# Two-layer graph network: edges of later windows from where their rows' own begin, fields from a table that ScalarE copies

## Chip, cores and metric

One core of one Trainium2 chip. The metric is the device time of one execution in microseconds, lower is better.

## What is computed

80,000 edges (src, dst, weight) join 2,500 nodes of 1,024 features. dst is sorted and dense at low numbers. Two layers, each with a layer norm in front:

```python
dst = jnp.minimum((2500 * uniform(80000) ** 2.0).astype(int32), 19999)   # then sorted
h = jnp.maximum(_layernorm(x, axis=-1), 0.0)
x = x + segment_sum((h @ W0)[src] * edge_weight[:, None], dst, 2500)
h = jnp.maximum(_layernorm(x, axis=-1), 0.0)
# layer 2: graph convolution with self loops, norm = deg**-0.5 [row] * deg**-0.5 [col], h2 = h @ W1.T + b
x = x + segment_sum(norm[:, None] * h2[col], row, 2500)
```

## The kernel before

Nothing is gathered by edge. Both layers multiply by matrices of nodes by nodes that the kernel builds itself: A with the sums of the weights of the edges from src to dst, and C with the counts of edges. They are built by matmuls of one-hot matrices. 128 edges make a *chunk* (625 of them, one edge a partition). A *window* is 4 rows of dst (640 windows, the last ones empty), 4 windows are a *quad* (160), 8 quads a tile of 128 rows (20). To *touch* a window with a chunk means one matmul of 128 by 128 by 240 columns: its left side marks for each edge which of the 128 (row, part of src) combinations of the window it has, its right side has the count and the two halves of the weight at the edge's place among 80. 8 touches are a *step*, with two buffers. A chunk belongs to a window only in part: what lies outside matches nothing.

How many chunks a window is touched with is fixed (`chunks_of`, `steps_of`): 32, 16, 8, 8 in quad 0, 8 in quads 1 to 3, 4 up to quad 31 (`UQ`), then 2 (`UL`). Where a window's edges reach over more chunks than that, `further` makes passes of 4 more chunks each, in a branch that the table `wtab` opens (first chunk, passes, passes before it, sum of the quad).

For a step of before:
- GpSimd, `fields` (L611, L613): for each window in turn it loads the first chunk from the table and copies the chunks' fields from `etab` (key, place, two halves of the weight) to `fbuf`, each twice, less the window's base. `sum_counts` (L627) adds the counts of a quad to the degrees.
- VectorE, `one_hots` (L863, L865, L868, L869): two comparisons with `iota_r` and two products.
- TensorE, `step` through `multiply` (L1379).
- ScalarE, `window_out` (L1154 to L1156), evacuates a quad from PSUM; VectorE, `second_part` (L920, L923), makes the low half of A.
- SyncE, `store_quad` (L413, L415), stores counts and both parts of A; `load_weights` (L424) loads a tile of A transposed, two DMAs, after the stores of all its quads.

There are two stages of this. First come the 20 *support* tiles (`support`, L1367, h @ W0, 48 products a tile), in which quads 0 to 15 are woven in from tile 4 on (`STEP0`, `STEPS_AT`: after which of the eight k-parts a step comes). VectorE, ScalarE and GpSimd have their order for a tile written out by hand; in tiles 4 to 7 ScalarE and GpSimd also split the second weights in blocks of which four belong to a tile (`W1_AT`, `split_block`, L1170, L1174, L636), stored by SP. Then 18 tiles of the aggregation (`dense`, L1433, 120 products of 512 columns a tile, 15 beside each quad) go with quads 16 to 159, which are two tiles ahead of their use. Two tiles are one turn of the loops of TensorE, VectorE and SyncE (two tiles are written out before them), one tile is a turn of ScalarE's. At a tile's start SP waits until the last quad is stored, then issues `load_weights`; the next quad's store is behind it in SP's queue, and ScalarE may evacuate a quad only when the store of the one two before has landed. TensorE may start a quad when the one two before is evacuated. VectorE's order in a quad is one-hots, second part of the quad before, `further`.

At the head VectorE makes the table for all 640 windows in nine passes on one partition (L822 to L832). L1460 spreads two fp32 rows over the partitions. L907 is the comparison of a further pass, L785 the low part of the support. After the loop come two tiles of aggregation without quads, and then the second layer (L1525, L1580), which the change doesn't touch.

## Time and profile before

| | |
|---|---|
| median of three runs | 1647.43 us (1643.34, 1647.43, 1656.27) |
| profiled execution | 1643.0 us |
| its span | 1641.3 us |
| TensorE busy | 1507.0 us (92%) |
| VectorE busy | 1064.6 us (65%) |
| GpSimd busy | 596.6 us (36%) |
| ScalarE busy | 443.1 us (27%) |
| support tiles end | at 334.3 us |
| last quad's step ends | at about 1010.4 us |

Busy times are of one execution. Matmuls are pipelined, so that a group's mean length is longer than its distance from one to the next. Times in the text without another word count from the span's start.

### The profile page before, as it was taken

The page shows a single profiled execution, that of the slowest core. Times are in us where ns is not written, and L with a number is a line of the kernel's source. Part 1 is how long each engine was busy: PE and PEld are TensorE (multiplying, and loading weights), DVE is VectorE, ACT ScalarE, POOL GpSimd, SP SyncE. Part 2 cuts the span into 40 slices and gives each one's busy share as a digit, 9 for nine tenths or more (in the row PEclk, how much of TensorE's full clock was granted, in tenths as well). Part 3 has the DMA queues.
Part 4 walks back from the last instruction along what each step waited for, and adds up shares of the span by engine and source line. Part 5 has one row for each costly group of instructions (what it writes and reads, how often), then busy time and mean ns, then how long its engine had stood idle before and what let it go on. Part 6 is the DMA issues. An engine that isn't in the chain of part 4 may idle for free.

```text
span 1641.3 us, 28252 instructions
## 1 busy us (share of the span) xinstructions
PE 1507.0 (92%) x7964; PEld 804.4 (49%) x7965; DVE 1064.6 (65%) x1917; ACT 443.1 (27%) x855; POOL 596.6 (36%) x1530
## 2 busy tenths in 40 slices
PE   3978999967889999999999999989999999999997
PEld 2444555534444545445444554334645545546455
DVE  5887764448867778778687785389555456355442
ACT  5745544312122222222222221171202103002000
POOL 1135543435656778667677774000000000000000
PEclk9989999988989999999999999999999999999999
DMA  7202421174556666656665656571331412403102
GB/s 279 104 26 68 147 58 33 25 157 97 110 119 142 151 146 139 143 131 157 136 151 130 151 135 160 180 281 32 125 102 51 120 56 89 128 11 122 55 1 75
DMA packets 411488, 185.71 MB, mean 113 GB/s; under 512 B 376875, under 2 KB 393791, under 8 KB 411342
## 3 DMA queue, kind: packets, MB, share of 16 engines
q1 hardware_dynamic: 411342, 184.03, 42.7%
q8 instruction: 59, 0.97, 0.2%
q14 instruction: 87, 0.71, 0.2%
HBM read 76.45 MB, written 77.11 MB: 94 GB/s over the span
## 4 chain that ended last, share of the span: by engine, by line
PE 58%; DVE 12%; SPq 9%; DMA 7%; issue 6%; ACT 3%; DVEq 1%; POOL 1%; ACTq 1%; POOLq 0%
PE pair L1525 20%; PE pair L1580 13%; PE pair L1367 9%; PE pair L1433 9%; SPq L424 6%; PE pair L1379 5%; DMA a_scratch<-area 5%; DVE slots L868 2%; DVE slots L865 2%; DVE slots L869 1%; DVE area L920 1%; DVE slots L863 1%; SPq L415 1%; SPq L445 1%; DMA wstage<-c_scratch 1%
## 5 line engine op out<-in xcount | busy, mean ns | idle before, releaser
L1433 PE MATMUL pair<-h,area 128*128 128x512 f16 x2400 | 548.1, 382 | 4.3 <-issue 3.9
L1433 PEld LDWEIGHTS pair<-h,area 128*128 128x128 f16 x2400 | 232.8, 98 | 266.1 <-issue 17.2
L1525 PE MATMUL pair<-area,h 128*128 128x500 f16 x1600 | 341.9, 376 | 6.4 <-DVE h L1042 6.4
L1379 PE MATMUL pair<-slots 128*128 128x240 f16 x1640 | 205.9, 272 | 76.6 <-DVE slots L869 58.8
L611 POOL CAST fbuf<-etab 128x12 f16 (+2 forms) x644 | 205.8, 320 | 174.6 <-DVE slots L869 106.6
L1525 PEld LDWEIGHTS pair<-area,h 128*128 128x128 f16 x1600 | 156.1, 98 | 191.5 <-issue 11.7
L1379 PEld LDWEIGHTS pair<-slots 128*128 128x128 f16 x1640 | 158.4, 99 | 138.6 <-DVE slots L869 65.6
L1154 ACT ACTIVATE area<-pair 128x320 f32<-128x320 f32 x160 | 69.9, 437 | 542.7 <-PE pair L1379 317.7
L613 POOL TENSOR_TENSOR fbuf<-etab,negbase 128x4 f16 (+3 forms) x644 | 211.0, 328 | 0.5 <-issue 0.5
L1580 PE MATMUL pair<-wmat,area 128*125 128x512 f16 x960 | 209.0, 379 | 0.0
L863 DVE TENSOR_TENSOR slots<-iota_r,fbuf 128x640 f16<-128x640 f16 x204 | 106.0, 519 | 142.9 <-POOL fbuf L613 85.4
L627 POOL TENSOR_TENSOR deg_acc<-deg_acc,area 128x320 f32<-128x320 f32 x160 | 145.0, 906 | 93.7 <-ACT area L1156 93.3
L1580 PEld LDWEIGHTS pair<-wmat,area 128*125 128x125 f16 x960 | 130.6, 136 | 75.5
L865 DVE TENSOR_TENSOR slots<-iota_r,fbuf 128x1024 f16<-128x1024 f16 x204 | 144.4, 708 | 0.0
L1309 ACT ACTIVATE area<-pair,sc 128x500 f16<-128x500 f32 x40 | 27.1, 677 | 385.2 <-PE pair L1525 385.2
L920 DVE SCALAR_TENSOR_TENSOR area<-pair,area 128x320 f16<-128x320 f32 x160 | 77.5, 484 | 81.9 <-ACT area L1156 81.6
L1367 PE MATMUL pair<-wmat,agg_t 128*128 128x512 f16 x480 | 112.7, 388 | 5.2 <-DVE wmat L778 4.0
L1082 DVE SCALAR_TENSOR_TENSOR area<-pair,sc,area 128x500 f16<-128x500 f32 x40 | 29.1, 738 | 128.3 <-ACT area L1309 128.2
L1367 PE MATMUL pair<-wmat,xt 128*128 128x512 f16 x480 | 110.0, 382 | 1.4 <-issue 1.4
L868 DVE TENSOR_TENSOR slots<-slots,fbuf 128x640 f16<-128x640 f16 x204 | 109.3, 536 | 0.0
L923 DVE TENSOR_TENSOR area<-area 128x320 f16<-128x320 f16 x160 | 101.4, 634 | 5.5
L869 DVE TENSOR_TENSOR slots<-slots,fbuf 128x640 f16<-128x640 f16 x204 | 104.1, 510 | 0.0
(195 smaller groups left out, 1117.5 us busy)
## 6 DMA issues: line engine op xcount, KB each, us to landing
c_scratch<-area SPq DMA_DIRECT2D x160, 160.0 KB, 2.3
a_scratch<-area SPq DMA_DIRECT2D x320, 80.0 KB, 2.3
xt<-x_scratch SPq DMA_DIRECT2D x20, 500.0 KB
out_x<-xt SPq DMA_DIRECT2D x20, 500.0 KB
xt<-in_x SPq DMA_DIRECT2D x19, 512.0 KB, 3.7
x_scratch<-xt SPq DMA_DIRECT2D x19, 512.0 KB, 3.3
wstage<-c_scratch SPq DMA_DIRECT2D x17, 500.0 KB, 4.5
slots<-c_scratch SPq DMA_DIRECT2D x17, 500.0 KB, 4.6
```

The lines of the kernel that those rows point to most:

```text
L611: pool.tensor_copy(fbuf[:, s, 1:F, at].rearrange("p f u d -> p u f d"), twice(etab_c[:, bass.ds(c, u), 1:F], [P, u, F - 1, 2])).then_inc(s ...
L613: pool.tensor_tensor(fbuf[:, s, 0, at], twice(etab_c[:, bass.ds(c, u), 0], [P, u, 2]), twice(negbase[:, bass.ds(v0 + w, 1)], [P, u, 2]), A ...
L627: pool.tensor_tensor(deg_acc[:], deg_acc[:], c_stage(s), ALU.add).then_inc(win_sum, 1)
L863: nc.vector.tensor_tensor(part(hot(s), M0, SB), columns(8, SB), by_touch(s, 1, 8, SB), ALU.is_equal).then_inc(hots_plain, 1)
L865: nc.vector.tensor_tensor(part(hot(s), 0, P), columns(8, P), by_touch(s, 0, 8, P), ALU.is_equal)
L868: nc.vector.tensor_tensor(part(hot(s), W0C, SB), part(hot(s), M0, SB), by_touch(s, 2, 8, SB), ALU.mult)
L869: nc.vector.tensor_tensor(part(hot(s), W1C, SB), part(hot(s), M0, SB), by_touch(s, 3, 8, SB), ALU.mult).then_inc(hots_ready, 1)
L1367: last = pe.matmul(dest[:, half * H:(half + 1) * H], h_t(t)[:, q, k, :], wmat[:, r, k, half * H:(half + 1) * H], start=k == q == r == 0, s ...
L1379: return pe.matmul(dest, touches[:, t, 0:P], touches[:, t, P:CS], start=first, stop=last, skip_group_check=True)
L1433: last = pe.matmul(sum_pair(e)[:, half * H:(half + 1) * H], wts(e)[:, q, k, :], hpart(k, r)[:, half * H:(half + 1) * H], start=k == q == r ...
L1525: ins = pe.matmul(sums_of(c, f), hpart(k, q)[:, f * P:(f + 1) * P], counts, start=first and q == 0, stop=last and q == 1, skip_group_check ...
L1580: last = pe.matmul(out_pair(m)[0:RW, half * H:(half + 1) * H], agg_of(k, q)[:, b * RW:(b + 1) * RW], wmat[:, r, k, half * H:(half + 1) * H ...
```

## The change

Windows of quads 16 to 63 are touched with 2 sets of 128 edges and those of quads 64 to 159 with 1, where the sets begin at the window's own first edge and not at a chunk's border: partition p takes the edge of the first chunk where that one is at or after the window's first row, and else that of the next chunk. A step is then one quad (16 to 63) or two (64 to 159). The fields of all these touches are made once, as a table `own` of 128 partitions by touches, four fields: matmuls of the edges' fields with one-hot matrices of the chunk numbers (`chunk_hot`, made at tile 6) give the fields of the second and third chunk and of the one that leads; VectorE chooses with predicated copies. TensorE does this in the support tiles named by `OWN_AT` and `SCRATCH_AT`, between its k-parts (`tables`), into TP; ScalarE copies TP out (`tables_out`) ahead of its weight blocks and of `window_out`; VectorE selects (`own_select`). A window with edges left over is forced out of the table and done by `further` passes alone (`select_windows`). The table of passes is made for 64 windows at the head and for the others at tile 16 (`later_windows`). In the loop ScalarE copies a step's fields from `own` into `fbuf`, in two copies of two fields each, a step ahead (`own_step`). GpSimd writes fields only for quads 0 to 15 and, at the head, makes three half-precision copies of the natural fields. The first `load_weights` moves from tile 12 to 17 of the support tiles. The loops of VectorE and TensorE are each two, up to quad 63 and from 64. The diff at its core:

```diff
-    U0, UH, UP, UL = (32, 16, 8, 8), 8, 4, 2
+    U0, UH, UP = (32, 16, 8, 8), 8, 4
     HQ = 4
     PRE = 2
     PQ = PRE * QPT
-    UQ = 4 * QPT
+    UA, UB, QB = 2, 1, 64
     BT = 4
     CS = P + 3 * SB
...
+    VA, VB = 4 * PQ, 4 * QB
+    NA = NW - VA
+    NT = UA * (VB - VA) + UB * (NW - VB)
+    V_HALF = (NA // 2, NA // 2)
...
+        ROW_AT, HOTS_AT, SELECT_AT, TABLE_AT = 5, 6, 9, 16
+        OWN_AT = {7: (0, 0), 8: (0, 1), 10: (1, 0), 11: (1, 1), 12: (2, 0), 13: (2, 1), 14: (3, 0), 15: (3, 1)}
+        SCRATCH_AT = sorted([ROW_AT, SELECT_AT, *OWN_AT])
...
-                if w == QPT:
+                if w + STEP0 == TABLE_AT + 1:
+                    sp.wait_ge(own_ready, len(OWN_AT))
+                    sp.wait_ge(table_ready, 2)
...
-            for t in range(4):
+            for t in range(2):
                 h_left(t)
-            for t in range(4, STEP0 + 2):
+            pool.wait_ge(scans_ready, 2)
+            pool.wait_ge(fields_ready, 2)
+            pool.tensor_copy(key_hi, field[0]).then_inc(nat_ready, 1)
+            pool.tensor_copy(from_h, field[1]).then_inc(nat_ready, 1)
+            pool.wait_ge(nat_ready, 1)
+            pool.tensor_tensor(key_lo, field[0], key_hi, ALU.subtract).then_inc(nat_ready, 1)
+            for t in range(2, STEP0 + 2):
...
-                    fields_of(w + 1)
+                    if w + 1 < PQ:
+                        fields_of(w + 1)
                     if w > 0:
                         sum_counts(w - 1, (w - 1) % 2)
-            for n in range(PQ, UQ):
-                if n + 1 < UQ:
-                    fields_of(n + 1)
-                else:
-                    step_loop(UQ, 0)
-                sum_counts(n - 1, (n - 1) % 2)
-            with pool.Fori(UQ // 2, NQ // 2 - 1) as i:
+            sum_counts(PQ - 1, 1)
+            with pool.Fori(PQ // 2, NQ // 2) as i:
                 for s in range(2):
-                    step_loop(i * 2 + s + 1, 1 - s)
-                    sum_counts(i * 2 + s - 1, 1 - s)
-            step_loop(NQ - 1, 1)
-            for n in range(NQ - 3, NQ):
-                sum_counts(n, n % 2)
+                    sum_counts(i * 2 + s, s)
 
             def self_loops(c, j):
 
...
+            def passes(a, b, count, cum, spare, start=None):
+
+                n = b - a
+                whole = spare[:, 0:n].bitcast(i32)
+                chain(nc.vector.tensor_scalar(whole, count, float(BT - 1), None, ALU.add))
+                chain(nc.vector.tensor_scalar(tab[:, 1, a:b], whole, 2, None, ALU.logical_shift_right))
+                chain(nc.vector.tensor_copy(spare[:, 0:n], tab[:, 1, a:b]))
+                chain(nc.vector.tensor_tensor_scan(cum, spare[:, 0:n], spare[:, 0:n], 0.0, ALU.add, ALU.bypass))
+                if start is not None:
+                    chain(nc.vector.tensor_scalar(cum, cum, start, None, ALU.add))
+                chain(nc.vector.tensor_scalar(tab[:, 3, a:b], cum, 1.0, None, ALU.add))
+                quads = spare[:, n:n + n // 4]
+                chain(nc.vector.tensor_reduce(quads, spare[:, 0:n].rearrange("o (g w) -> o g w", w=4), AX.X, ALU.add))
+                chain(nc.vector.tensor_copy(tab[:, 3, a:b].rearrange("o (g w) -> o w g", w=4)[:, 0, :], quads))
+                nc.vector.tensor_tensor(tab[:, 2, a:b], cum, spare[:, 0:n], ALU.subtract).then_inc(table_ready, 1)
+
             dve.wait_ge(wrow_in, 16 * NB)
-            lo_row = wrow.rearrange("o (v a) -> o a v", a=2)[:, 0, 0:NW]
-            n_row = wrow.rearrange("o (v a) -> o a v", a=2)[:, 1, 0:NW]
-            tab = wtab.rearrange("o (v a) -> o a v", a=4)
-            cum = wcum[:, 0:NW]
-
-            chain(nc.vector.tensor_scalar(wint[:, 0:NW], n_row, float(BT - 1), None, ALU.add))
-            chain(nc.vector.tensor_scalar(tab[:, 1, :], wint[:, 0:NW], 2, None, ALU.logical_shift_right))
-            chain(nc.vector.tensor_copy(n_row, tab[:, 1, :]))
...
+            def own_hots(k, s, used):
+                dve.wait_ge(own_fields, 2 * (k - PRE_STEPS) + 2)
+                one_hots(k, s, used)
...
+                    if chunks == UA:
+                        own_hots(n + PRE_STEPS - PQ, q % 2, n - 1 + PRE_STEPS - PQ)
+                    elif q % 2 == 0:
+                        own_hots((td + PRE) * 4 + q // 2 + QB // 2 + PRE_STEPS - PQ, q // 2 % 2, steps_used(n - 2))
...
+            def own_select(t):
+
+                f, half = OWN_AT[t]
+                at = slice(half * V_HALF[0], (half + 1) * V_HALF[0])
+                dve.wait_ge(own_copied, scratch_uses(t) + 1)
+                two = VB - VA if half == 0 else 0
+                pairs = own[f][:, 0:UA * two].rearrange("p (v u) -> p u v", u=UA)
+                singles = own[f][:, UA * (VB - VA):NT][:, 0 if half == 0 else V_HALF[0] - (VB - VA):]
+                singles = singles[:, 0:V_HALF[0] - two]
+                lead = from_lead[:, 0:V_HALF[0]]
+                mask = from_first[:, at]
+                if f == 0:
+                    chain(nc.vector.tensor_scalar(mask, lead, 0.0, None, ALU.is_ge))
+                    for chunk, a, b in ((pairs[:, 1], 0, two), (singles, two, V_HALF[0])):
+                        if a < b:
+                            out = left_over[:, at][:, a:b]
+                            chain(nc.vector.scalar_tensor_tensor(out, chunk, 0.0, mask[:, a:b], ALU.is_ge, ALU.mult))
+                            chain(nc.vector.scalar_tensor_tensor(out, chunk, P / 2, out, ALU.is_lt, ALU.mult))
+                    if half == 0:
+                        chain(nc.vector.tensor_scalar(sums_row, tab[:, 1, VA:NW], -1.0, 0.0, ALU.add, ALU.max))
+                    rest = left_over[0:1, at]
+                    nc.vector.tensor_tensor(rest, rest, sums_row[:, at], ALU.add).then_inc(left_ready, 1)
+                if two:
+                    nc.vector.copy_predicated(singles, mask[:, two:V_HALF[0]], lead[:, two:V_HALF[0]])
+                    chain(nc.vector.copy_predicated(pairs[:, 1], mask[:, 0:two], pairs[:, 0]))
+                    last = nc.vector.copy_predicated(pairs[:, 0], mask[:, 0:two], lead[:, 0:two])
+                else:
+                    last = nc.vector.copy_predicated(singles, mask, lead)
+                last.then_inc(own_ready, 1)
+
+            def select_windows():
+
+                dve.wait_ge(own_copied, scratch_uses(SELECT_AT) + 1)
...
+            def select_windows():
+
+                dve.wait_ge(own_copied, scratch_uses(SELECT_AT) + 1)
+                dve.wait_ge(own_ready, 2)
+                chain(nc.vector.tensor_scalar(forced, forced, 0.0, 50000.0, ALU.is_gt, ALU.mult))
+                pairs = own[0][:, 0:UA * (VB - VA)].rearrange("p (v u) -> p u v", u=UA)
+                for u in range(UA):
+                    nc.vector.scalar_tensor_tensor(pairs[:, u], pairs[:, u], 10000.0, forced[:, 0:VB - VA],
+                                                   ALU.min, ALU.add)
+                singles = own[0][:, UA * (VB - VA):NT]
+                chain(nc.vector.scalar_tensor_tensor(singles, singles, 10000.0, forced[:, VB - VA:NA], ALU.min, ALU.add))
+                for u, a, b in ((UA, 0, VB - VA), (UB, VB - VA, NA)):
+                    chain(nc.vector.tensor_scalar(sums_row[:, a:b], tab[:, 1, VA + a:VA + b], float(u), None, ALU.add))
+                chain(nc.vector.scalar_tensor_tensor(sums_row, forced[0:1, :], 0.0, sums_row, ALU.is_gt, ALU.mult))
+                chain(nc.vector.tensor_copy(tab[:, 1, VA:NW], sums_row))
+
+            def later_windows():
+                chain(nc.vector.tensor_copy(wcum[:, 0:NA], tab[:, 1, VA:NW]))
+                passes(VA, NW, wcum[:, 0:NA], wcum[:, 0:NA], wtmp, top[0:1, 10:11])
 
             hots_of(0)
...
+                if w + STEP0 == HOTS_AT:
+                    chunk_one_hots()
+                if w + STEP0 in OWN_AT:
+                    own_select(w + STEP0)
+                if w + STEP0 == SELECT_AT:
+                    select_windows()
+                if w + STEP0 == TABLE_AT:
+                    later_windows()
...
+            with dve.Fori(1, ONE_FROM) as i:
                 tile(i, 0)
                 tile(i, 1)
+
+            dve.wait_ge(step_used, steps_used(QB - 1))
+            with dve.Fori(ONE_FROM, T // 2 - 1) as i:
+                tile(i, 0, UB)
+                tile(i, 1, UB)
             chain(nc.vector.tensor_reduce(sel[:], ident[:].rearrange("p (r k) -> p k r", r=R), AX.X, ALU.add))
...
+            def own_step(k, s):
+
+                act.wait_ge(hots_ready, k - 1)
+                at = bass.ds((k - PRE_STEPS) * 8, 8)
+                act.activation(fbuf[:, s, 0:2], twice(own_k[:, :, at], [P, 2, 8, 2]), ACT.Copy).then_inc(own_fields, 1)
+                act.activation(fbuf[:, s, 2:4], twice(own_w[:, :, at], [P, 2, 8, 2]), ACT.Copy).then_inc(own_fields, 1)
+
+            def tile(td, chunks=UB, last=False):
                 for q in range(QPT):
                     n = QPT * (td + PRE) + q
-                    window_out(n, q % 2, steps_before(n + 1))
+                    if chunks == UA:
+                        own_step(n + 1 + PRE_STEPS - PQ, 1 - q % 2)
+                    elif q % 2 == 0 and not (last and q == QPT - 2):
+                        own_step((td + PRE) * 4 + q // 2 + 1 + QB // 2 + PRE_STEPS - PQ, 1 - q // 2 % 2)
+                    window_out(n, q % 2, steps_used(n + 1))
 
...
+            def tables_out(t):
+
+                act.wait_ge(own_sums, scratch_uses(t) + 1)
+                if t not in OWN_AT:
+                    dest = chunk_row if t == ROW_AT else forced
+                    act.activation(dest[:, 0:512], TP[:, 0:512], ACT.Copy)
+                    act.activation(dest[:, 512:NA], TP[:, 512:NA], ACT.Copy).then_inc(own_copied, 1)
+                    return
+                f, half = OWN_AT[t]
+
+                need(act, own_ready, own_at(t) - 1)
+                n, two = V_HALF[half], VB - VA if half == 0 else 0
+                act.activation(from_lead[:, 0:n], TP[:, 0:n], ACT.Copy)
+                if two:
+                    pairs = own[f][:, 0:UA * two].rearrange("p (v u) -> p u v", u=UA)
+                    act.activation(pairs[:, 1], TP[:, n:n + two], ACT.Copy)
+                    act.activation(pairs[:, 0], TP[:, H:H + two], ACT.Copy)
+                a = UA * (VB - VA) + (0 if half == 0 else V_HALF[0] - (VB - VA))
+                act.activation(own[f][:, a:a + n - two], TP[:, H + two:H + n], ACT.Copy).then_inc(own_copied, 1)
+
...
+            act.wait_ge(table_ready, 2)
+            act.wait_ge(own_ready, len(OWN_AT))
+            own_step(PRE_STEPS, 0)
+            with act.Fori(0, QB // QPT - PRE) as td:
+                tile(td, UA)
+            with act.Fori(QB // QPT - PRE, T - PRE - 1) as td:
                 tile(td)
-            with act.Fori(UQ // QPT - PRE, T - PRE) as td:
-                tile(td)
...
+            def own_step(k, s, u, pair, half=0):
+
+                pe.wait_ge(hots_ready, k + 1)
+                for t in range(4 * u):
+                    last = multiply(hot(s), half * 4 + t, win(pair, t // u), first=t // u % 2 == t % u == 0,
+                                    last=t % u == u - 1)
+                last.then_inc(step_used, 1)
+
...
+            def tables(t):
+
+                if t + 1 < T:
+                    pe.wait_ge(ht_ready, 2 * t + 4)
+
+                need(pe, own_copied, scratch_uses(t))
+                if t == ROW_AT:
+                    pe.wait_ge(wrow_in, 16 * NB)
+                    pe.matmul(TP[:, 0:512], ones[0:1, :], lo_row[:, VA:VA + 512], start=True, stop=True)
+                    pe.matmul(TP[:, 512:NA], ones[0:1, :], lo_row[:, VA + 512:NW], start=True,
+                              stop=True).then_inc(own_sums, 1)
+                    return
+                if t == SELECT_AT:
+                    pe.wait_ge(left_ready, 2)
+                    pe.matmul(TP[:, 0:512], ones_h, left_over[:, 0:512], start=True, stop=True)
+                    pe.matmul(TP[:, 512:NA], ones_h, left_over[:, 512:NA], start=True, stop=True).then_inc(own_sums, 1)
+                    return
+                f, half = OWN_AT[t]
+                pe.wait_ge(chunk_hots, 1)
+                pe.wait_ge(nat_ready, 3)
+                n = V_HALF[half]
+                at = half * V_HALF[0]
+                two = VB - VA if half == 0 else 0
+                for g, dest, width in ((0, TP[:, 0:n], n), (1, TP[:, H:H + n], n), (2, TP[:, n:n + two], two)):
+                    if not width:
+                        continue
+                    if f == 0:
+                        pe.matmul(dest, ones_h[0:1, :], neg_row[:, at:at + width], start=True, stop=False)
+                    for i, by_chunk in enumerate(own_parts[f]):
+                        for j in range(J):
+                            last = pe.matmul(dest, by_chunk[:, j * P:(j + 1) * P], chunk_hot[:, j - g + 2, at:at + width],
+                                             start=f > 0 and i == j == 0, stop=i == len(own_parts[f]) - 1 and j == J - 1)
+                last.then_inc(own_sums, 1)
+
             def further(n, pair):
...
+                    if k == 5 and t in SCRATCH_AT:
+                        tables(t)
...
+            with pe.Fori(0, ONE_FROM) as i:
+                tile(i, 0, UA)
+                tile(i, 1, UA)
+            with pe.Fori(ONE_FROM, T // 2 - 1) as i:
+                tile(i, 0, UB)
+                tile(i, 1, UB)
```

## Rows read from the trace of the kernel before

**Rows 1.** The page's first line: the span and its instructions
```profile
span 1641.3 us, 28252 instructions
```

**Rows 2.** Windows by stage: start:end and length, busy us (records) per engine, clock, DMA
```profile
193.30:334.30 141.00, 141.00 (x865) 77.72 (x863) 70.63 (x151) 64.02 (x97) 54.85 (x108) 1.00 0.18 38
334.30:471.10 136.80, 104.28 (x593) 58.51 (x593) 100.56 (x206) 23.00 (x62) 70.88 (x192) 0.89 0.59 128
...
588.00:1010.40 422.40, 396.53 (x2219) 212.68 (x2217) 321.96 (x625) 105.20 (x288) 300.78 (x854) 1.00 0.63 143
```

**Rows 3.** Groups by line: count, busy us and mean ns, idle before them
```profile
L1379 PE MATMUL pair<-slots 128*128 128x240 f16 x1640 | 205.9, 272 | 76.6 <-DVE slots L869 58.8 <-DVE area L920 6.6 <-DVE slots L912 6.1
...
L865 DVE TENSOR_TENSOR slots<-iota_r,fbuf 128x1024 f16<-128x1024 f16 x204 | 144.4, 708 | 0.0
...
L863 DVE TENSOR_TENSOR slots<-iota_r,fbuf 128x640 f16<-128x640 f16 x204 | 106.0, 519 | 142.9 <-POOL fbuf L613 85.4 <-issue 34.5 <-PE pair L1379 19.8
...
L1460 PE MATMUL pair<-area,ones 1*128 1x512 f32 (+1 forms) x8 | 4.3, 716 | 3.7 <-ACT etab L1227 3.7
...
L825 DVE TENSOR_TENSOR_SCAN area<-area 1x640 f32<-1x640 f32 x1 | 1.5, 1478 | 0.0
...
L907 DVE TENSOR_TENSOR slots<-iota_r,fbuf 128x512 f16<-128x512 f16 x2 | 0.9, 426 | 0.0
```

**Rows 4.** TensorE in order of time, the loop: start us, length us
```profile
550.26 0.98 PE L1379 MATMUL pair<-slots 128*128 128x240 f16 x8
...
554.31 0.98 PE L1379 MATMUL pair<-slots 128*128 128x240 f16 x8
555.13 3.40 PE L1433 MATMUL pair<-h,area 128*128 128x512 f16 x15
...
575.48 0.99 PE L1379 MATMUL pair<-slots 128*128 128x240 f16 x8 [0.72 <-DVE slots L869]
...
588.05 0.98 PE L1379 MATMUL pair<-slots 128*128 128x240 f16 x8
...
611.83 0.99 PE L1379 MATMUL pair<-slots 128*128 128x240 f16 x8 [1.80 <-DVE slots L869]
```

**Rows 5.** Chain of waits, 720 to 800: start us, length us, what
```profile
728.51 3.87 issue
...
768.71 0.37 SPq L413
...
772.05 2.80 SPq L424
...
774.99 2.90 SPq L424
...
779.28 2.33 DMA a_scratch<-area
...
786.63 0.99 PE pair L1379 x8
```

**Rows 6.** TensorE in order of time, from the loop's first tiles
```profile
341.00 3.36 PE L1379 MATMUL pair<-slots 128*128 128x240 f16 x16 [6.57 <-DVE area L920]
...
376.07 3.51 PE L1379 MATMUL pair<-slots 128*128 128x240 f16 x16 [13.04 <-DVE slots L869]
...
455.48 0.98 PE L1379 MATMUL pair<-slots 128*128 128x240 f16 x4 [6.07 <-DVE slots L912]
```

**Rows 7.** SyncE's queue in order of time, same stretch
```profile
351.44 16.16 SPq L445 DMA_TRANSPOSE wmat<-w_scratch  x2
```

**Rows 8.** TensorE in order of time, support tiles
```profile
93.03 2.75 PE L1367 MATMUL pair<-wmat,agg_t 128*128 128x512 f16 x12 [1.19 <-DVE h L785]
...
185.91 1.78 PE L1379 MATMUL pair<-slots 128*128 128x240 f16 x8 [3.41 <-DVE slots L869]
```

**Rows 9.** ScalarE in order of time, support tile 5
```profile
133.41 0.70 ACT L1170 ACTIVATE h<-h,sc 128x512 f32<-128x512 f32 x1
```

**Rows 10.** VectorE in order of time, a late support tile
```profile
306.82 0.49 DVE L863 TENSOR_TENSOR slots<-iota_r,fbuf 128x640 f16<-128x640 f16 x1 [7.07 <-POOL fbuf L613]
```

175 lines of the change are left out of this document (105 added, 70 removed).

## The prediction

> **What bounds the kernel now.** I read the windows by stage first, then the groups by line, then TensorE's order of time, and last the chain of waits inside one tile. The page's own execution spans 1641.3 us [rows 1] and took 1643.0 us, so what lies around the span is 1.7 us. The median of the three runs shown is 1647.43, 4.4 above it. TensorE (PE) is the engine to follow. In support tiles 8 to 19 it is busy for all of 141.00 us [rows 2]: whatever is added on PE there is added to the time. From 334.3 to 471.1, where quads 16 to 35 are done, it is busy 104.28 of 136.80 us [rows 2]: here other things bound it. A step is 8 matmuls of 240 columns. The groups show 1640 of them [rows 3]: 204 steps, and 2 further passes of 4.
>
> In the loop a quad costs PE 0.82 us for the step and 3.24 us for 15 products: steps start at 550.26, 554.31, and the products begin at 555.13 [rows 4]. Pure pace would be 4.06 us a quad. But from the last quad of a tile (554.31) to the fifth of the next (575.48) it takes 21.17 us, not 5 x 4.06 = 20.3, and the next time (588.05 to 611.83) 23.78 us [rows 4]. The chain of waits tells why [rows 5]: the last quad's store is issued at 768.71, then two transposing loads hold the SP queue 2.80 and 2.90 us, only then goes the next quad's store, which lands after 2.33 us; ScalarE's evacuation of the third quad has waited for that landing, VectorE's second part and the one-hots for the fifth quad follow it, and PE starts at 786.63. The last quad's step had begun some 21.2 us before that. None of this chain is made shorter by fewer matmuls. In the other tile of each pair VectorE also pays 3.87 us of "issue" as its loop goes back [rows 5].
>
> **The change part by part.**
>
> *Fewer steps.* Before: 44 steps up to quad 15, 2 x 16 for quads 16 to 31, 128 for the rest, 204. After: 44 + 48 (quads 16 to 63) + 48 (one step for two quads, 64 to 159) = 140. It takes away 64 steps: 52 us of PE at 0.82 us, and on VectorE 64 times some 2 us (519 and 708 ns for the two comparisons [rows 3], and two products of the first one's size, which overlap a little). How much of that is on the path is told by stage.
>
> *Quads 16 to 35.* The stage is 136.80 us [rows 2]. (a) PE first stands 6.57 us before 341.00 [rows 6]; VectorE has then made both steps' one-hots of quad 16 before it finishes quad 15. With one step this is 1.6 to 2.0 us less; I take 1.6. (b) Then SP issues the transposes, the two of the second weights alone 16.16 us from 351.44 [rows 7], and PE stands 13.04 us before 376.07 [rows 6]. That chain keeps its length; it ends 1.6 earlier, at 374.4. PE comes to it sooner and waits longer, for nothing gained. (c) From there before goes at 5.5 to 6 us a quad, VectorE-bound with two steps each (2 x 2 us and the second part). After, it goes as the later loop does: three quads of 4.06 and about 1.5 for the cold clock, 388.1; one chain of 21.2, three quads, one more chain: quad 36 begins at 442.7, against 471.1 before. (d) In this is a further pass: the row of 4 matmuls at 455.48 had PE idle 6.07 us [rows 6], and only two such passes are in the trace (L907, x2 [rows 3]), one in quad 0, which stays. The reference's own inputs give at most 222 edges in a window of quads 16 to 63 and 113 in one of quads 64 and up, so that 256 and 128 slots counted from the window's own first edge hold them: no later pass is left. Sum: 28.4 us less. Bounds: 18 (if only (a), the pass and half of the VectorE time come off) and 34.
>
> *Quads 36 to 63.* Same steps, same chain. GpSimd's copies no longer run beside VectorE's one-hots, and ScalarE gets two 32-element copies a quad, which I put at 0.2 us each (a third to a half of its 320-element copy); it waits most of the time. They are queued ahead of the evacuation of the quad before, and they wait for one-hots that are one quad older, which are done. The cover is ScalarE's idle time; without it each quad would be 0.4 us longer. Change 0, bounds -4 and +6.
>
> *Quads 64 to 159.* A quad falls from 4.06 to 3.65 us (half a step). Outside the chain there are three quads a tile, 12 tiles: 36 x 0.41 = 14.8 us less. Inside the chain nothing: five quads now need only 18.25 us and PE stands 3 us in a 21.2 us chain. Where VectorE's loop goes back the chain starts by VectorE's clock, and the last quad's step is now 0.41 us later with respect to it, so it takes about 24.5: 5 x 0.65 = 3.3 us more. One of the old back-branches (quad 63 to 64) becomes the passage from one loop into the next, which I take as 2.7 us less. That is 14.2 us less. Against it stand PE's longer idle times. After 3.41 us of idling the 8 matmuls at 185.91 took 1.78 us instead of 0.98 [rows 4, 8]: TensorE's 1.2 GHz level instead of 2.4. Tiles at the back-branch would have gaps of 2.3 and 4.0 us; I charge 1.1 us in each of 5: 5.5. Net 9 us less. Bounds: 15 less, and with 1.6 us in all 12 tiles, 5 more.
>
> By the Trainium skill (Runtime: NRT & Kernel Launch, section Instruction fetch mechanics) a taken branch to a page outside the two held ones must fetch it first, and straight running does not. The trace agrees in so far as VectorE's long loop shows 3.87 us at its start. By that rule falling out of one loop into the next costs nothing; were it wrong, the 2.7 us would go and the sum be 14.
>
> *Tiles 4 to 19, what is added.* The tables are made by one-hot matmuls in TP: 22 x 288 + 11 x 192 columns for support tile 7, 22 x 288 for 8, then 3 x (20 x 288 + 5 x 192) for 10 to 15, 34,944 columns. At 0.82 us for 8 x 240 columns [rows 4] that is 14.9 us, of it 3.6 in tile 7, 2.7 in 8 and 8.6 in 10 to 15; 0.3 in 9. Tile 5 has 576 fp32 columns at the rate of L1460, whose eight records take 4.3 us for 1250 columns [rows 3]: 2.0 us. These sums stand on PE in the stage where it is never idle. More comes from ScalarE's order. It reads the tables after PE's sixth part of the tile, and its blocks of the second weights (tiles 4 to 7) stand behind that. In tile 5 the blocks began at 133.41 [rows 9]. Now ScalarE must wait for PE to about 139.1 and copy to 139.9, 6.5 us later; GpSimd, the next fields and PE follow, about 4.8 us of it reaching PE. In tile 7 it waits for 3.6 us of matmuls as well, so that PE's second step of tile 8, at 185.91 before [rows 8], comes some 10.6 us late. With tile 8's own 2.7, 0.3 and 8.6 it is 22 us.
> VectorE's selects, one-hots of chunk numbers and the later windows' table are hidden: it idles 7.07 us in such a tile [rows 10], the largest block (nine passes over 576 elements on one partition, of which the scan is 1478 ns for 640 [rows 3]) some 9 us, with 3 to 4 us of slack at PE. In tiles 10 to 15, though, the select waits for ScalarE's copy near the end of the tile and two one-hot sets stand behind it; I find only about 1 us to spare there. Every us more would be PE's in up to 8 tiles.
> At the head the table of the first 64 windows replaces one of 640, about 6 us less on VectorE, but PE waited for it only 1.19 us at 93.03 [rows 8]: about 2 less. Net 20 us more; bounds 11 (the PE columns of tiles 8 to 15 alone) and 45.
>
> **Sum.** -28.4 + 0 - 9 + 20 = -17: 1643.0 - 17 = 1626 against the profiled execution, 1630 against the median. I say 1628.
>
> **The rivals.** About 1% is what a measurement of this kernel tells from no change.
> 1. *The tables hold the support tiles up.* VectorE's select, behind ScalarE's copy, makes the next one-hots late, 3 us in each of 8 tiles (24 us), and the wait in tile 7 is longer by 5; also the idle times cost the clock in every late tile (nothing gained there). 20 + 29 - 28 + 0 = 21 more: 1664. For it: 1 us of slack by my count, and an order with four engines in it. Against: VectorE's 7.07 us idle. It decides from about 2.5 us a tile. 0.15.
> 2. *What is saved late is eaten by waits and the clock.* PE's time in quads 64 to 159 doesn't change, since the chain through the transposes is what counts, and the tables cost 25: -28 + 25 = -3, 1640. For it: [rows 5]. 0.27.
> 3. *The chain shrinks with the load.* If with GpSimd out the stores and the second part come sooner and PE alone sets the pace, quads 64 to 159 take 96 x 3.65 = 350 us plus 6 stalls of 2.3 instead of the 422.40 of [rows 2]: 1643 + 20 - 28 - 58 = 1577. Against: every link of it is on SP, DMA and ScalarE, and stays. 0.05.
> 4. *It doesn't do what it says*: windows overflow and take further passes, 8 to 10 us each as at 455.48. The counts above exclude it nearly: 0.01.
> My forecast has 0.52.
>
> **How the numbers follow.** The forecast's own range is 1612 to 1643; taking in most of rival 2 and the bounds of the tables' cost, 1603 to 1655. The forecast lies at the 1% mark, and a little over half of it and all of rival 3 are beyond: faster 0.46; same 0.39; slower 0.15 from rival 1.
>
> **What would show it.** Right: 140 steps (1124 matmuls of 240 columns with the pass that stays), one L907 pass, no GpSimd casts after tile 19; the support tiles 8 to 19 ending about 20 us later; quad 36 about 8 us earlier than before; 39 us less matmul time in quads 64 to 159, but more idling of PE there, and the stretch from a tile's last quad to the next one's fifth still 21 to 25 us. Wrong: support tiles longer than 14.5 us each (rival 1), a stretch under 20 us (rival 3), or ScalarE late with the fields, seen as VectorE waiting for it ahead of the one-hots.

## The result, and the profile after

The changed kernel takes 1671.27 us (median of four runs, 1666.7 to 1672.5) against 1648.75 for the kernel before (median of four): a ratio of 1.0136, with a 95% interval of [1.0111, 1.016]. I had said 1628, in 1603 to 1655. It is slower, and outside the range. The profiled execution took 1672.5 us.

The first lines of the page of the changed kernel:
```profile
span 1670.7 us, 24358 instructions
## 1 busy us (share of the span) xinstructions
PE 1496.5 (90%) x7584; PEld 776.4 (46%) x7585; DVE 953.0 (57%) x1710; ACT 472.7 (28%) x1075; POOL 262.9 (16%) x384
```
The work did shrink: VectorE from 1064.6 to 953.0 us, GpSimd from 596.6 to 262.9. The span grew by 29.4 us.

Windows by stage of the kernel before, where quads 36 to 63, quads 64 to 159 and the rest are cut apart (columns as in [rows 2]); [rows 2] has the two stages ahead of them:
```profile
471.10:593.40 122.30, 115.35 (x645) 61.82 (x643) 91.46 (x179) 30.68 (x84) 88.52 (x250) 1.00 0.62 139
593.40:1009.40 416.00, 391.25 (x2185) 209.65 (x2186) 320.01 (x621) 104.11 (x285) 298.95 (x847) 1.00 0.63 143
1009.40:1641.30 631.90, 612.90 (x2871) 318.16 (x2869) 335.69 (x495) 113.13 (x173) 15.21 (x25) 0.99 0.30 97
```
And of the changed kernel, support tiles 8 to 19, quads 16 to 35, 36 to 63, 64 to 159, the rest:
```profile
193.30:360.20 166.90, 161.80 (x1003) 91.30 (x1003) 100.31 (x210) 72.36 (x123) 51.89 (x115) 0.98 0.23 58
360.20:472.10 111.90, 87.18 (x461) 46.47 (x460) 67.96 (x135) 28.07 (x106) 18.34 (x20) 0.88 0.70 151
472.10:601.90 129.80, 120.06 (x644) 63.49 (x645) 94.33 (x182) 37.13 (x140) 27.87 (x28) 0.96 0.58 134
601.90:1037.10 435.20, 374.28 (x1807) 179.30 (x1806) 220.81 (x427) 114.64 (x377) 85.98 (x95) 0.94 0.61 137
1037.10:1670.70 633.60, 612.12 (x2867) 317.61 (x2865) 335.83 (x495) 113.25 (x173) 14.46 (x25) 0.99 0.30 97
```

| stage | before | after | difference | forecast |
|---|---|---|---|---|
| support tiles end | 334.3 | 360.2 | +25.9 | +20 |
| quads 16 to 35 | 136.8 | 111.9 | -24.9 | -28.4 |
| quads 36 to 63 | 122.3 | 129.8 | +7.5 | 0 |
| quads 64 to 159 | 416.0 | 435.2 | +19.2 | -9 |
| the rest | 631.9 | 633.6 | +1.7 | 0 |

The largest miss is where I expected a gain. In quads 64 to 159 TensorE's busy time fell by only 17 us (391.25 to 374.28), not by the 39 of 48 steps, and its granted clock from 1.00 to 0.94. The groups by line in that stretch, kernel before:
```profile
L1433 PE MATMUL pair<-h,area 128*128 128x512 f16 x1425 | 323.3, 379 | 2.5 <-issue 2.1
L1379 PE MATMUL pair<-slots 128*128 128x240 f16 x760 | 93.7, 266 | 23.4 <-DVE slots L869 23.3
...
L865 DVE TENSOR_TENSOR slots<-iota_r,fbuf 128x1024 f16<-128x1024 f16 x95 | 64.9, 684 | 0.0
```
and changed kernel (L1649 are the products of the aggregation, L1553 the steps, L919 the larger comparison):
```profile
L1649 PE MATMUL pair<-h,area 128*128 128x512 f16 x1426 | 342.7, 395 | 7.5 <-issue 7.5
...
L1553 PE MATMUL pair<-slots 128*128 128x240 f16 x381 | 57.6, 276 | 53.4 <-DVE slots L923 53.4
...
L919 DVE TENSOR_TENSOR slots<-iota_r,fbuf 128x1024 f16<-128x1024 f16 x47 | 38.7, 824 | 0.0
```
The steps cost 36 us less, but the idle time before them grew by 30 (23.4 to 53.4), and the same products, none added, took 19 us more (323.3 to 342.7). TensorE in order of time shows both at one place, the fifth quad of a tile, changed kernel:
```profile
721.14 0.57 PE L1553 MATMUL pair<-slots 128*128 128x240 f16 x4
721.55 3.40 PE L1649 MATMUL pair<-h,area 128*128 128x512 f16 x15
728.54 0.98 PE L1553 MATMUL pair<-slots 128*128 128x240 f16 x4 [3.58 <-DVE slots L923]
729.86 5.77 PE L1649 MATMUL pair<-h,area 128*128 128x512 f16 x15 [0.34 <-issue]
735.47 0.57 PE L1553 MATMUL pair<-slots 128*128 128x240 f16 x4
735.88 3.40 PE L1649 MATMUL pair<-h,area 128*128 128x512 f16 x15
```
A quad goes at 3.65 us as forecast (0.41 for half a step and 3.24 for the products). Then TensorE stands 3.58 us, and the 15 products behind the pause take 5.77 us, where they take 3.40 elsewhere: most of them at the 1.2 GHz level. It idles 3.2 to 4.2 us at the fifth quad of each of the 12 tiles, and 1.5 to 1.9 us where the loop goes back. From the fifth step to the sixth it takes 5.3 to 7.0 us. That is 1.7 to 3.4 us over the pace, in every tile. From 728.50 to 735.40 the granted clock is 0.55 of full speed, from 735.40 to 742.00 it is 1.00. Behind the 1.5 to 1.9 us at the loop's turn the 15 products take 3.41 us, as elsewhere.

What it waits for is the chain I had read in [rows 5], in the same place, changed kernel's chain of waits:
```profile
712.86 2.90 SPq L470
...
715.89 2.82 SPq L470
...
720.11 3.08 DMA a_scratch<-area
...
724.00 0.45 ACT area L1290
724.48 0.50 DVE area L982
...
726.33 0.17 DVE slots L919
726.50 1.10 issue
...
728.08 0.41 DVE slots L923
728.49 0.05 issue
728.54 0.98 PE pair L1553 x4
```
Two transposing loads, the next quad's store, ScalarE's evacuation, VectorE's second part and one-hots, the step. The last quad's step before the loads to the fifth quad's step: 21.6 to 22.2 and 24.7 to 25.2 us in the two kinds of tile (without and with the jump back of VectorE's loop), where it was 21.3 to 21.5 and 23.7 to 24.4 in the kernel before. The chain is a little longer, and the work beside it is less. Two of its links grew. The comparison of L919 takes 1.35 us (0.17 and the 1.10 of issue behind it in this view, until the next one can start) where L865 took 0.68. And in the tiles without the jump the store behind the two loads lands after 3.0 to 3.1 us (3.08 above) where it took 2.3 to 2.4 (2.33 in [rows 5]); with the jump it takes 2.0 to 2.1 in both kernels. Why that store became slower is open.

### The profile page after: what moved, and what is told of

Same layout as the page of the kernel before. It is cut to its first block, busy times and chain, and to the rows that moved or that the text cites. A ratio compares the mean times of both kernels' runs of the same rounds, so it can differ in the third digit from the quotient of the medians.

```text
span 1670.7 us, 24358 instructions
## 1 busy us (share of the span) xinstructions
PE 1496.5 (90%) x7584; PEld 776.4 (46%) x7585; DVE 953.0 (57%) x1710; ACT 472.7 (28%) x1075; POOL 262.9 (16%) x384
## 4 chain that ended last, share of the span: by engine, by line
PE 60%; SPq 10%; DVE 9%; DMA 8%; issue 7%; ACT 4%; DVEq 1%; ACTq 1%; POOL 0%; POOLq 0%
PE pair L1744 20%; PE pair L1799 12%; PE pair L1541 10%; PE pair L1649 10%; SPq L470 6%; DMA a_scratch<-area 5%; PE pair L1553 4%; DVE area L982 1%; DVE slots L922 1%; DVE slots L923 1%; SPq L461 1%; DVE slots L919 1%; SPq L459 1%; DMA wstage<-c_scratch 1%; SPq L493 1%
## 5 line engine op out<-in xcount | busy, mean ns | idle before, releaser
L1649 PE MATMUL pair<-h,area 128*128 128x512 f16 x2400 | 571.4, 394 | 9.1 <-issue 9.0
L1649 PEld LDWEIGHTS pair<-h,area 128*128 128x128 f16 x2400 | 240.0, 101 | 288.6 <-issue 55.2
L1553 PE MATMUL pair<-slots 128*128 128x240 f16 x1124 | 152.4, 276 | 110.3 <-DVE slots L923 93.3
L1553 PEld LDWEIGHTS pair<-slots 128*128 128x128 f16 x1124 | 109.9, 100 | 165.8 <-DVE slots L923 112.8
L917 DVE TENSOR_TENSOR slots<-iota_r,fbuf 128x640 f16<-128x640 f16 x140 | 74.5, 532 | 92.7 <-issue 54.4
L919 DVE TENSOR_TENSOR slots<-iota_r,fbuf 128x1024 f16<-128x1024 f16 x140 | 110.1, 786 | 0.0
L985 DVE TENSOR_TENSOR area<-area 128x320 f16<-128x320 f16 x160 | 76.9, 481 | 5.5
L923 DVE TENSOR_TENSOR slots<-slots,fbuf 128x640 f16<-128x640 f16 x140 | 75.5, 540 | 0.0
L1541 PEld LDWEIGHTS pair<-wmat,agg_t 128*128 128x128 f16 x480 | 47.8, 101 | 57.2 <-issue 10.0
L922 DVE TENSOR_TENSOR slots<-slots,fbuf 128x640 f16<-128x640 f16 x140 | 74.1, 529 | 0.0
L1541 PEld LDWEIGHTS pair<-wmat,xt 128*128 128x128 f16 x480 | 46.7, 99 | 53.9 <-issue 4.2
```

The lines of the kernel that those rows point to most:

```text
L919: nc.vector.tensor_tensor(part(hot(s), 0, P), columns(8, P), by_touch(s, 0, 8, P), ALU.is_equal)
L922: nc.vector.tensor_tensor(part(hot(s), W0C, SB), part(hot(s), M0, SB), by_touch(s, 2, 8, SB), ALU.mult)
L923: nc.vector.tensor_tensor(part(hot(s), W1C, SB), part(hot(s), M0, SB), by_touch(s, 3, 8, SB), ALU.mult).then_inc(hots_ready, 1)
L985: nc.vector.tensor_tensor(a_stage(s)[:, 1], a_stage(s)[:, 1], a_stage(s)[:, 2], ALU.add).then_inc(win_lo, 1)
L1541: last = pe.matmul(dest[:, half * H:(half + 1) * H], h_t(t)[:, q, k, :], wmat[:, r, k, half * H:(half + 1) * H], start=k == q == r == 0, s ...
L1553: return pe.matmul(dest, touches[:, t, 0:P], touches[:, t, P:CS], start=first, stop=last, skip_group_check=True)
```

## The experiments

Late stage means quads 64 to 159. Each ratio is to the kernel before as timed beside that run; 2 and 11 are edits of the kernel before, all others of the changed one. Idle is TensorE's idle time before steps in it, and a product's mean length is that of the 512-column products there.

| kernel | median us | ratio | late stage us | idle us | product ns |
|---|---|---|---|---|---|
| before | 1646 to 1649 | 1 | 416.0 | 23.4 | 379 |
| changed | 1671.27 | 1.0136 | 435.2 | 53.4 | 395 |
| 1 more products ahead of the wait | 1637.44 | 0.9932 [0.9909, 0.9955] | 406.8 | 33.3 | 387 |
| 2 the same in the kernel before | 1648.08 | 1.0001 [0.999, 1.0012] | | | |
| 3 steps' matmuls twice | 1675.04 | 1.0167 [1.015, 1.0185] | 438.9 | 33.1 | 388 |
| 4 weight blocks first | 1654.04 | 1.0037 [1.0019, 1.0055] | 435.6 | | |
| 5 degrees cut | 1650.31 | 1.0023 [1.0007, 1.0039] | 425.5 | 42.8 | 395 |
| 6 no copies | 1668.42 | 1.013 [1.01, 1.0161] | 435.5 | 49.6 | 399 |
| 7 one-hots a quad earlier | 1619.21 | 0.9842 [0.9813, 0.9871] | 383.7 | 21.1 | 386 |
| 8 idle time filled | 1652.57 | 1.0038 [1.0024, 1.0052] | 417.4 | 14.5 | 384 |
| 9 experiments 4 and 7 | 1605.77 | 0.9748 [0.9731, 0.9764] | | | |
| 10 one-hots early in all quads | 1600.69 | 0.9723 [0.9706, 0.9739] | 389.9 | 25.3 | 387 |
| 11 one-hots early in the kernel before | 1702.94 | 1.0346 [1.0327, 1.0365] | | | |
| 12 and the loop's end | 1586.34 | 0.9632 [0.9616, 0.9648] | 380.8 | 17.7 | 385 |

**1 and 2. Another division of the products over the quads.** Quads 0 to 3 of a tile get 18 of the 120 products, 4 to 6 get 10, the last 18, so that there is more work for TensorE while the chain runs. Once in the changed kernel (1), once in the kernel before (2).

```diff
-        SUMS_AT = [15 * q for q in range(QPT + 1)]
+        SUMS_AT = [0, 18, 36, 54, 72, 82, 92, 102, 120]
```

> The changed kernel with the 120 products of a tile divided 18, 18, 18, 18, 10, 10, 10, 18 over its eight quads in place of 15 each: work moves into the five quads that lie in the stretch from a tile's last quad to the next tile's fifth, out of the three behind it. Theory A (the stretch of 22 to 25 us is set by the chain through store and transposes, TensorE idles 3.4 to 4.2 us in it and then runs products at the 1.2 GHz level): the idling goes, the clock stays up, and a pair of tiles in quads 64 to 159 goes from 73.2 us to about 62 to 65; 1671 becomes 1580 to 1610. Theory B (the late stage is slower because each quad waits for ScalarE's copies and VectorE, and the idling costs nothing by itself): a quad with more products is only longer, the pair stays at 71 to 75 and the time within 1% of 1671.

> The kernel before with the same division of the products. Theory A: here TensorE idles only about 1 to 2 us in the stretch and has 32.5 us of its own work in a tile of 35; it gains less, 1 to 2 us a tile, 15 to 35 us in all, and ends up slower than the changed kernel with the same division. Theory B: no gain, and the changed kernel stays behind it by the 20 to 25 us of now.

Measured: the changed kernel gains 34 us by it, the kernel before nothing (1648.08, ratio 1.0001 [0.999, 1.0012]). With this division the order of the two turns round: the changed one is 11 us ahead. So a good part of the loss is waiting that work from elsewhere in the tile can fill. Both gains are smaller than theory A had them (to 1580 to 1610, and 15 to 35 us for the kernel before). In both kernels the idle time moved to the first quad of the loop's turn (in the kernel before TensorE stood 3.24 us before 594.69 and 3.71 before 666.47, in the changed one 3.30 to 3.69 us at that place), with a slow stretch behind it; why it moved there I didn't follow further.

**3. The removed matmuls put back.** The steps of quads 64 to 159 do their 4 matmuls a quad twice.

```diff
-                for t in range(4 * u):
+                for t in list(range(4 * u)) * (2 if u == UB else 1):
```

> The changed kernel with the four matmuls of each quad from 64 on done twice over (the first of a bank starts its sums anew, so the sums are the same): the matmuls that the change took away come back, 96 x 0.41 = 39 us of TensorE, all else stays. Theory A: they fill the wait, TensorE idles about 1.5 to 2 us at a tile's fifth quad in place of 3.5 to 4.2, keeps 2.4 GHz more often, and quads 64 to 159 take 420 to 430 us in place of 435: with 4 x 96 more matmuls the kernel is 5 to 15 us faster. Theory B, or if the clock costs nothing: 36 quads lie outside the stretch and cost 0.41 each, 15 us slower.

Measured: 39 us of matmuls came back, and the late stage grew by 3.7 us (435.2 to 438.9). A tenth of their length: nine tenths of what the change takes from TensorE there lay in waits and in slow products. The time is 3.8 us longer, between the two expectations (5 to 15 us faster, 15 slower).

The run says more than that. In this stage it has all the matmuls of the kernel before (2185 records on TensorE in both), and still takes 438.9 us where that kernel takes 416.0. So it isn't the missing matmuls that make the late stage longer than before: to take them away in the changed kernel gains 3.7 us. Something else in the change costs 22.9 us beside them; experiment 5 has a part of it.

**4. ScalarE's weight blocks ahead of its table copies.**

```diff
-                if t in SCRATCH_AT:
-                    tables_out(t)
...
                     split_block(g)
+                if t in SCRATCH_AT:
+                    tables_out(t)
```

> The changed kernel with ScalarE's copies of the tables behind its blocks of the second weights instead of ahead of them, in support tiles 5 and 7. Theory A (of the 25.9 us that the support stage grew, about 11 are ScalarE standing in front of the blocks until TensorE has made the tables, the rest TensorE's own columns): support ends 8 to 12 us earlier, 1659 to 1664. Rival (the growth is TensorE's columns and VectorE's selects): within 3 us of 1671.

Measured: 17.2 us less, and the support tiles end at 347.0 instead of 360.2. Support tiles 8 to 19 in it, to be held against the 166.90 above and the 141.00 of [rows 2]:
```profile
193.30:347.00 153.70, 153.26 (x960) 86.54 (x958) 88.20 (x190) 70.06 (x120) 44.81 (x101) 1.00 0.17 36
```
That is more than expected (13.2 us at the support tiles' end for 8 to 12, and 1654 us for 1659 to 1664). TensorE has no pause above 0.4 us left in it, and what remains over the kernel before, 12.7 us, is near the 11.6 us of table columns that I had put into tiles 8 to 15 (2.7 + 0.3 + 8.6).

**5. GpSimd's degrees cut.** From quad 16 on GpSimd adds 2 of the 80 columns of the counts to the degrees; the other columns are left out.

```diff
-                    sum_counts(i * 2 + s, s)
+                    n = i * 2 + s
+                    pool.wait_ge(win_act, n + 1)
+                    pool.wait_ge(win_sum, n)
+                    pool.tensor_tensor(deg_acc[:, :, 0:2], deg_acc[:, :, 0:2], c_stage(s)[:, :, 0:2],
+                                       ALU.add).then_inc(win_sum, 1)
```

> The changed kernel with GpSimd's addition of a quad's counts to the degrees cut to 2 of 80 columns from quad 16 on (it leaves out nearly all of the degrees, so the second layer is not the reference's; the load there stays). Theory C (GpSimd, rid of the fields, now adds the counts in the very moment in which VectorE makes the fifth quad's one-hots, so that the second comparison takes 1.38 us instead of 0.68 and the chain through a tile's start is about 1 us longer than before; this pushes TensorE's idling over what its clock bears): the chain shortens by about 1 us, TensorE idles 2.5 to 3 us instead of 3.5 to 4, and with less loss of clock the kernel is 20 to 45 us faster than 1671. If the addition doesn't matter: within 5 us.

Measured: 21 us less in all, 9.7 of it in the late stage and some 9 before quad 64. The reason is in the order of time, changed kernel, at the fifth quad:
```profile
726.21 0.92 POOL L681 TENSOR_TENSOR deg_acc<-deg_acc,area 128x320 f32<-128x320 f32 x1 [0.83 <-ACT area L1290]
726.27 0.96 SPq L461 DMA_DIRECT2D a_scratch<-area  x2
726.33 1.35 DVE L919 TENSOR_TENSOR slots<-iota_r,fbuf 128x1024 f16<-128x1024 f16 x1
```
VectorE's comparison begins 0.12 us behind GpSimd's addition and takes 1.35 us, where it takes 687 ns in the mean in experiment 5 and 684 in the kernel before. The Trainium skill (SBUF — State Buffer, section Who interferes with whom) says that a VectorE instruction with two inputs in SBUF contends with a GpSimd instruction that reads SBUF, and that the ports they share are an exclusive lock. The trace agrees roughly: the comparison ends some 0.55 us after the addition does, a little less than the 0.68 us that it takes alone. I had only seen that GpSimd's casts go from beside VectorE. I hadn't seen what else follows: without them the addition starts as soon as ScalarE's evacuation ends (0.1 us behind it here), right in front of the one-hots that TensorE waits for, while in the kernel before, in the tile of [rows 5], it started at 786.87, 2.2 us behind the evacuation and after the one-hots. The cut addition also lets VectorE's subtraction in the second part (L985) take 325 ns in the mean instead of 511.

The steps' times give the late stage in two terms: the 12 stretches from a tile's last quad to the next one's fifth, and the three quads behind each, with what these take over TensorE's pace (12 x 3 x 4.06 us with 8 matmuls a quad, 12 x 3 x 3.65 with 4):

| kernel | stretches us | three quads behind us | of it over the pace | both |
|---|---|---|---|---|
| before | 271.8 | 149.6 | 3.4 | 421.4 |
| 3, matmuls put back | 280.9 | 162.2 | 16.0 | 443.2 |
| 5, degrees cut | 268.0 | 161.6 | 30.2 | 429.6 |
| changed | 278.6 | 160.6 | 29.2 | 439.2 |

In experiment 5 the stretches are no longer than in the kernel before, and with 39 us less of matmuls it is still 8.2 us slower: there less work beside the chain does cost more than it saves. With the longer stretches (experiment 3 against the changed kernel) the same removal gains 4.0. And the longer stretches alone (kernel before against experiment 3) cost 21.8 us, of which 9.1 are their own length and 12.6 come behind them. So each of the two, the longer chain and the missing work, opens pauses that cost more than their length, and the costs don't add. It isn't a clean square: experiment 5 also shortens the second part, and in it, as in experiment 3, the store behind the loads still takes 3.0 to 3.1 us.

**6. ScalarE's copies taken out.** The two copies of fields a step become a bare signal; the fields of quads 16 and later are left out with them.

```diff
-                act.activation(fbuf[:, s, 0:2], twice(own_k[:, :, at], [P, 2, 8, 2]), ACT.Copy).then_inc(own_fields, 1)
-                act.activation(fbuf[:, s, 2:4], twice(own_w[:, :, at], [P, 2, 8, 2]), ACT.Copy).then_inc(own_fields, 1)
+                act.sem_inc(own_fields, 2)
```

> The changed kernel without ScalarE's two copies of a step's fields (only their signal is left; every step of quads 16 to 159 works with old fields, so the sums are not the reference's). Theory B (ScalarE's copies, ahead of its evacuations, lengthen the chain): 10 to 30 us faster than 1671. Theory C and the idle theory: the copies lie in ScalarE's own waiting, at most 5 us faster.

Measured: 1668.42, ratio 1.013 [1.01, 1.0161], within the interval of the changed kernel's own; late stage 435.5. The copies cost nothing that can be told from noise.

**7. The one-hots out of the chain.** From quad 64 VectorE makes the one-hots of a pair of quads a quad earlier, ahead of the second part that waits for the chain.

```diff
-                    elif q % 2 == 0:
-                        own_hots((td + PRE) * 4 + q // 2 + QB // 2 + PRE_STEPS - PQ, q // 2 % 2, steps_used(n - 2))
+                    elif q % 2 == 1 and not (last and q == QPT - 1):
+                        own_hots((td + PRE) * 4 + (q + 1) // 2 + QB // 2 + PRE_STEPS - PQ, (q + 1) // 2 % 2,
+                                 steps_used(n - 1))
...
+            own_hots(QB + PRE_STEPS - PQ, 0, steps_used(QB - 1))
```

> The changed kernel with VectorE making the one-hots of the next two quads one quad earlier (from quad 64 on), ahead of the second part that waits for the landed store, instead of behind it. Chain theory: 2.0 to 2.8 us drop out of every stretch from a tile's last quad to the next tile's fifth, 12 times, and TensorE's idling there sinks from about 3.8 to 1 to 1.5 us, below what costs the clock: 30 to 55 us faster than 1671, that is 1616 to 1641. If the stretch is bound by something else (PSUM, the store's landing alone): under 10 us.

Measured: 52 us less, late stage 383.7. Idle before steps falls from 53.4 to 21.1, and only one pause a pair of tiles is left, now for the second part:
```profile
749.09 0.58 PE L1556 MATMUL pair<-slots 128*128 128x240 f16 x4 [3.71 <-DVE area L982]
749.96 5.00 PE L1652 MATMUL pair<-h,area 128*128 128x512 f16 x15 [0.28 <-issue]
```

**8. The idle time filled with useless work.** From quad 64 the first quad of each tile does its 15 products twice: 12 x 15 products, 39 us.

```diff
-                for k, q, r, half in list(sum_products())[SUMS_AT[g]:SUMS_AT[g + 1]]:
+                these = list(sum_products())[SUMS_AT[g]:SUMS_AT[g + 1]]
+                for at, (k, q, r, half) in enumerate(these * (2 if again else 1)):
...
-                    dense(i, e, g)
+                    dense(i, e, g, chunks == UB and g == 0)
```

> The changed kernel with the 15 products of each tile's first quad done twice over from quad 64 on (the second time they start the sums anew, so the result is the same): 3.24 us more of TensorE work a tile, put where it stands idle later. Idle theory (TensorE's idling at the fifth quad is free to fill, and drops its clock to 1.2 GHz for the next 15 or so products at 1.7 to 3 us): the added work costs nothing and the clock stays up, 12 tiles times 1 to 2.5 us: 10 to 30 us faster than 1671. If the clock is lost anyway, or the time is TensorE's own: 0 to 39 us slower.

Measured: 18.7 us faster than the changed kernel, with 39 us of matmuls more. The groups of its late stage and TensorE around a fifth quad:
```profile
L1650 PE MATMUL pair<-h,area 128*128 128x512 f16 x1606 | 368.4, 384 | 6.7 <-issue 6.7
...
L1553 PE MATMUL pair<-slots 128*128 128x240 f16 x380 | 55.0, 268 | 14.5 <-DVE slots L923 14.3
```
```profile
692.09 3.40 PE L1650 MATMUL pair<-h,area 128*128 128x512 f16 x15
696.48 0.58 PE L1553 MATMUL pair<-slots 128*128 128x240 f16 x4 [0.98 <-DVE slots L923]
```
The pause at the fifth quad is 0.98 us here, where the changed kernel has 4.14 in the same tile; in the other tiles it is shorter or gone, but for one of 2.54 us. The mean product takes 384 ns instead of 395, the granted clock of the stage is 0.98 instead of 0.94. Idle time before steps fell by 38.9 us, just what was added, and TensorE's busy time rose by only 21.9 us (374.28 to 396.17): the rest of the matmuls took 17 us less, nearly the 17.8 us by which the stage is shorter. If only the chain had counted, filling it would have changed nothing; that the time falls is the part of the clock. So the late stage's loss has two parts which this run takes apart: the chain, which swallows what the change saves, and the slow products behind the pauses, which cost about 17 us on top. Experiment 3 filled the same stretches with five quads' share of its 39 us; the share of the other three, 14.8 us, lies outside them and costs its length, and so its sum is a loss.

**9. Experiments 4 and 7 together.**

> The changed kernel with both: ScalarE's blocks of the second weights ahead of its copies of the tables (as e4, -17) and the one-hots a quad earlier from quad 64 on (as e7, -52). They act in different stages, so chain theory: they add up, 1671 - 17 - 52 = 1602, within 6. If part of either was the same gain (the state of the clock, a shifted phase): 1607 to 1619.

Measured 1605.77, within the 6 us of the first expectation: 65.5 us less than the changed kernel, for 17.2 + 52.1 = 69.3 alone.

**10. The same for quads 16 to 63.** Kernel 9 with one-hots a quad early in those quads too, fields two steps ahead, and the second part of quad 15 ahead of quad 16's one-hots.

```diff
+                    if first and q == 0:
+                        second_part(n - 1, 1 - q % 2, True)
+                        own_hots(PRE_STEPS, 0, steps_used(n - 1))
                     if chunks == UA:
-                        own_hots(n + PRE_STEPS - PQ, q % 2, n - 1 + PRE_STEPS - PQ)
+                        own_hots(n + 1 + PRE_STEPS - PQ, 1 - q % 2, n + PRE_STEPS - PQ)
...
-                        own_step(n + 1 + PRE_STEPS - PQ, 1 - q % 2)
+                        own_step(n + 2 + PRE_STEPS - PQ, q % 2)
```

> As e9, with the one-hots a quad earlier in quads 16 to 63 too (fields copied two steps ahead, and the second part of quad 15 ahead of the first one-hots). Chain theory: there the stretch is 23 to 25 us with TensorE's own 20.3, so 1.5 to 3 us drop out in 5 tile starts, with the clock kept, and 2 us at the first store: 8 to 18 us below e9. Rival (ScalarE's and VectorE's longer runs ahead make nothing shorter there, since quads of 8 matmuls fill the stretch anyway): within 4 us of e9.

Measured 1600.69: 5 us below experiment 9, less than for the late quads, and between the two expectations (8 to 18, and within 4).

**11. The same order in the kernel before.** Is it the order alone, without the table?

```diff
-                    else:
-                        one_hots(steps_before(n), q % 2, windows_to(n, 0))
+                    elif not (last and q == QPT - 1):
+                        one_hots(steps_before(n + 1), 1 - q % 2, windows_to(n + 1, 0))
```

> The kernel before with VectorE's one-hots made a quad earlier, ahead of the waiting second part, from quad 32 on (the edit of e7 and e10 without the change). Chain theory: here TensorE has 4.06 us a quad and stands only 0.7 to 1.8 us a stretch without loss of clock, so there is little to win: about 1 us in each of 16 tile starts, 10 to 25 us, to 1622 to 1637. If e7's gain were not the change's but would come to the old kernel as well: 1595 to 1610, as low as e9.

Measured: 1702.94, ratio 1.0346 [1.0327, 1.0365], 57 us slower. Both expectations missed. The waits of this kernel from 588 to 1067.9 (engine, line, releaser: us, times, longest):
```profile
ACT area L1157 <- DMA a_scratch<-area: 371.1, 100, 9.4
POOL deg_acc L627 <- ACT area L1159: 135.1, 56, 7.2
DVE slots L863 <- POOL fbuf L613: 84.0, 62, 4.4
```
VectorE now stands 84 us in front of its one-hots for fields that GpSimd hasn't written yet, and the second part stands behind it; the store and ScalarE's evacuation follow late (in the kernel before ScalarE waited for stores 155.8 us in nearly the same quads, here 371.1). TensorE's pauses grow to up to 4.2 us, and its granted clock in the window falls to 0.96. By this reading the early order needs fields that are there early, which GpSimd's order of work doesn't give and the change's table does; it is read from the waits, and no run tests it by itself.

**12. The loop's end.** Kernel 10, with the second part of a pair of tiles' last quad moved from the head of VectorE's loop body to its end, so that it doesn't stand behind the jump back.

```diff
-                    if not (first and q == 0):
+                    if not (first and q == 0) and not (q == e == 0):
                         second_part(n - 1, 1 - q % 2)
...
+                    if q == QPT - 1 and e == 1:
+                        second_part(n, q % 2)
```

> e10 with the second part of a pair of tiles' last quad done at the end of VectorE's loop body instead of behind its jump back: the 3.75 us of issue at the jump no longer stand between the last quad and its store. Chain theory: in 7 of the stretches 3 to 4 us of TensorE's idling and the low clock behind it go, a pair of tiles in quads 64 to 159 falls from 65 to about 60 to 62 us: 1601 becomes 1570 to 1585. If the stretch there is set by TensorE's waiting for the one-hots or by the loads: within 5 us of e10.

Measured: 1586.34 us (1584.76 to 1588.15), ratio 0.9632 [0.9616, 0.9648], the fastest here, 5.1% under the changed kernel, and 14 us under experiment 10; the expectation was 1570 to 1585. Its page's first lines, the window of its late stage, and TensorE at two fifth quads there:
```profile
span 1586.4 us, 24308 instructions
## 1 busy us (share of the span) xinstructions
PE 1474.0 (93%) x7584; PEld 772.2 (49%) x7585; DVE 957.4 (60%) x1710; ACT 473.4 (30%) x1075; POOL 265.3 (17%) x384
```
```profile
571.60:952.40 380.80, 359.13 (x1807) 175.94 (x1806) 221.49 (x428) 115.17 (x378) 84.62 (x96) 0.98 0.72 157
```
```profile
658.49 0.58 PE L1561 MATMUL pair<-slots 128*128 128x240 f16 x4 [1.53 <-DVE area L982]
659.35 5.10 PE L1657 MATMUL pair<-h,area 128*128 128x512 f16 x15 [0.28 <-issue]
...
722.28 0.58 PE L1561 MATMUL pair<-slots 128*128 128x240 f16 x4 [2.05 <-DVE area L982]
723.14 3.41 PE L1657 MATMUL pair<-h,area 128*128 128x512 f16 x15 [0.28 <-issue]
```
A pause of 2.05 us here leaves the next 15 products at 3.41, while behind one of 1.53 us they take 5.10. TensorE has as many records as in the changed kernel (7584) and 22.5 us less busy time: the same matmuls at a higher clock.

## Why the prediction was wrong, and where it was right

**Quads 64 to 159: the step that failed is "I charge 1.1 us in each of 5".** I had the chain, its 21.2 us, that five quads need only 18.25 beside it, and even that TensorE falls to the 1.2 GHz level after 3.41 us of idling [rows 8]. I gave that to the tiles at the back-branch alone. But the pauses at the fifth quad are 3.2 to 4.2 us in all 12 tiles, and the cost behind each is 1.7 to 3.4 us. Even my bound ("with 1.6 us in all 12 tiles, 5 more") charged too little. Second in the same step: "Inside the chain nothing". It did grow. By the sums behind experiment 5, from quad 63's step to quad 159's: the three quads outside give back 14.8 us by their pace, as forecast; what they take over the pace rose by 25.8 us (3.4 to 29.2), where I had 5.5; and the stretches rose by 6.8 us (271.8 to 278.6), where I had 3.3 - 2.7 = 0.6. That is 17.8 more for the forecast's 9 less. (The stage of the table above begins one step later; the step from quad 63 to 64 took 5.37 us before and 4.06 after, which makes it 19.2.) Of the stretches' growth the runs show two links, GpSimd's addition in front of the comparison (experiment 5) and the slower store; I had looked for neither. And the account must not stop at the missing matmuls: put back, they leave the stage 22.9 us longer than before (experiment 3).

**Quads 36 to 63: "Change 0, bounds -4 and +6".** It was +7.5, with the clock down from 1.00 to 0.96: the same kind of pause, three of 2.1 to 2.8 us (at 508.13, 528.77 and 583.95), each with 15 products of 4.7 to 5.1 us behind it; in the kernel before the longest is 1.80 us and no products are slow. These quads have all their matmuls, so here it is the longer chain alone. I had reckoned with GpSimd's casts gone from beside VectorE as the only change there. How much of it is the degrees' addition, the rest of the chain (the slower store) or the clock isn't divided; experiment 5 took some 9 us from the quads before 64, so its part is large. The copies, priced at 0.2 us each (240 ns measured), are hidden, as I had said: experiment 6.

**Tiles 4 to 19: +25.9 for +20.** The columns were right: with ScalarE's order out of the way (experiment 4) 12.7 us remain against 11.6. The mis-sized term was that order, "some 10.6 us late" for TensorE's second step of tile 8. TensorE in order of time, changed kernel:
```profile
194.76 1.23 PE L1553 MATMUL pair<-slots 128*128 128x240 f16 x8 [3.86 <-DVE area L982]
199.19 1.78 PE L1553 MATMUL pair<-slots 128*128 128x240 f16 x8 [3.20 <-DVE slots L923]
```
That is 13.3 us later than 185.91 [rows 8]. ScalarE stood for the tables 5.07 us in tile 5 and 8.04 in tile 7, and its blocks began at 138.47 (5.1 later, 6.5 forecast) and at 182.33 instead of 168.17 in tile 7. The 2 us that I took off at the head for the smaller table don't show in the sum.

**Quads 16 to 35: -24.9 for -28.4.** Right in kind and nearly in size. The waits of [rows 6] stayed: 5.06 us for 6.57 at the first step (1.5 less, 1.6 forecast), and SP's two loads of the second weights hold its queue 16.63 us for the 16.16 of [rows 7]; TensorE stands 16.41 us for them instead of 13.04, and goes on 1.8 us earlier from the stage's start than before, where I had 1.6. The missing 3.5 us lie behind that wait: 71.9 us from there to quad 36, forecast 68.3. The further pass is gone, and the trace has the 1124 matmuls of 240 columns that I had counted.

**The loop cut in two.** The passage from quad 63 to 64 takes 22.24 us from the last step (597.88) to the fifth (620.12), like a tile without a back-branch (21.6 to 22.2) and not one with (24.7 to 25.2). The Trainium skill (Runtime: NRT & Kernel Launch, section Instruction fetch mechanics) has only a taken branch to a page that isn't held stall for its fetch; this passage agrees. Experiment 12 used the same 3 to 4 us from the other side.

**The rivals.** Rival 2, what is saved late is eaten by waits and the clock, named the mechanism; its 1640 came from taking "eaten" as the worst. The chain is a floor for the waits but none for the clock: less work or a longer chain makes longer pauses, and behind longer pauses the remaining work was slower, so the sum can pass zero. I had no case for that: the 0.15 for slower hung on rival 1. Rival 1, late selects in the late support tiles, didn't happen: these take 14.1 and 14.5 us and TensorE waits in them at most 0.44 us; its time was nearest (1664), for another reason. Rivals 3 and 4 are excluded: no stretch is under 21 us, and the 1124 matmuls leave no room for further passes. The chance of "faster", 0.46, doesn't follow from its own words either: a little over half of 0.52 and 0.05 make about 0.33.

## What to carry to other kernels

Where a chain of waits sets a stretch, taking work off the busy engine beside it isn't worth its length, and may be worth less than nothing: price the pauses that it opens, and the lower clock behind each, in every turn of the loop, before counting the saving. Ask as well which links of the chain the change makes longer: here a chain longer by under 1 us a tile cost more than the missing work (21.8 us with all matmuls in place, experiment 3). Then look what in the chain needn't be there: here the one-hots stood behind a waiting instruction only by the order of VectorE's program, and moving them (experiment 7) turned a loss of 1.4% into a gain of 1.6%. A change which makes data available early pays when the order is changed to use it; the same order with the old late data (experiment 11) lost 3.5%.

## What the runs showed of the hardware

- In a stream that is otherwise dense, pauses of TensorE of 3.2 to 4.2 us were followed by 15 products of 512 columns that took 4.3 to 5.9 us instead of 3.40. After one of 2.05 us (experiment 12) they took 3.41, but in experiment 1, after one of 2.02 us, 10 products took 3.46 instead of 2.32, and in experiment 12, after one of 1.53 us, 15 took 5.10. In the kernel before, none of the pauses of 0.8 to 1.9 us in the late stage had slow products behind it. The length of the pause alone doesn't tell.
- Useless matmuls, 39 us of them put where TensorE would idle, made the kernel 18.7 us faster.
- Which engine is freed decides when the other one is hit: behind GpSimd's 128 x 320 addition, no longer late, VectorE's comparison is 1.35 us long instead of 0.68, on the path, and cutting the addition brought 21 us.
- A store of one quad behind two transposing loads landed after 3.0 to 3.1 us in the changed kernel and 2.3 to 2.4 in the kernel before, in the same kind of tile. The cause is open.
